# Bulk loads issued by GpSimd, one transposing DMA per attention step, and a column of ones in V

## The reference

```python
x = x + attention(layernorm(x), Wq, bq, Wk, bk, Wv, bv)
x = x + (layernorm(x) @ (weight * scale[:, None]).T + bias)
```

```python
scores = einsum('nhbqd,nhbkd->nhbqk', qb, kb) / sqrt(d)     # local windows
ctx    = einsum('nhbqk,nhbkd->nhbqd', softmax(scores), vb)
_, top_idx = top_k(norm(q), 62);  idx = concat([0, top_idx, t - 1])
ctx[idx] = softmax(q[idx] @ k.T / sqrt(d)) @ v
```

## Time and profile before

| | |
|---|---|
| median of 3 runs | 2244.83 us (2239.55 to 2246.85) |
| the profiled execution | 2241.47 us, span 2239.5 us |
| TensorE busy | 2039.9 us, 91% |
| VectorE, ScalarE, GpSimd busy | 1524.9, 1047.0, 523.3 us |
| attention of the second batch, 600 to 986 us | 386.0 us, TensorE busy 337.06, granted clock 0.92 |
| attention of the fourth batch and what follows, 1530 to 1880 us | 350.0 us, TensorE busy 317.29, granted clock 0.93 |
| linear layer, 1880 to 2239 us | 359.0 us, TensorE busy 355.61, granted clock 1.00 |

### The profile page before, as it was taken

How to read it: one execution, slowest core, us unless ns; L and a number is a source line. 1 busy time by engine, 2 the same in 40 slices (tenths; PEclk the granted TensorE clock), 3 DMA queues, 4 the chain that set the end, 5 groups by cost and what they waited for, 6 DMA issues and landing times.

```text
span 2239.5 us, 37450 instructions
## 1 busy us (share of the span) xinstructions
PE 2039.9 (91%) x11264; PEld 1698.9 (76%) x11264; DVE 1524.9 (68%) x2904; ACT 1047.0 (47%) x1979; POOL 523.3 (23%) x336
## 2 busy tenths in 40 slices
PE   6989797999988879999888699998998997999999
PEld 6877685787867767888677578886887876888887
DVE  6687675774876757748777577577785775666664
ACT  4325555683256646742465466624675682000000
POOL 2241121123321121132321312233222202212221
PEclk9999898999989989999999899999999998999999
DMA  4346656654365566643465556524666645333331
GB/s 154 91 103 132 143 123 117 137 121 130 88 146 129 134 114 124 132 130 113 110 135 138 118 132 132 123 83 97 138 142 169 153 78 166 141 131 127 136 140 66
DMA packets 539680, 280.73 MB, mean 125 GB/s; under 512 B 439120, under 2 KB 504726, under 8 KB 539536
## 3 DMA queue, kind: packets, MB, share of 16 engines
q1 hardware_dynamic: 531888, 261.21, 49.0%
q10 hardware_dynamic: 4320, 15.73, 1.7%
q0 software_dynamic: 3328, 2.17, 0.5%
HBM read 122.73 MB, written 51.44 MB: 78 GB/s over the span
## 4 chain that ended last, share of the span: by engine, by line
PE 47%; DVE 18%; DMA 11%; ACT 9%; issue 8%; SPq 6%; DVEq 1%; ACTq 0%; POOL 0%; POOLq 0%
PE proj L639 20%; PE proj L799 15%; DMA p_turned<-p_parts 7%; PE pv L757 4%; ACT pT L1127 4%; SPq L295 3%; DVE x_norm L1454 3%; ACT probs L1105 3%; DVE top_val L1450 2%; DVE p_parts L1496 2%; DVE top_idx L1452 2%; PE score L771 2%; DVE q_sq L1416 2%; DMA stat_rows<-ln_rstd 1%; PE pv L779 1%
## 5 line engine op out<-in xcount | busy, mean ns | idle before, releaser
L639 PE MATMUL proj<-xT_hi,w_hi 128*128 128x512 f32 x1536 | 447.2, 438 | 99.5 <-ACT vT L1075 79.9
L639 PEld LDWEIGHTS proj<-xT_hi,w_hi 128*128 128x128 f32 x1536 | 302.5, 207 | 169.3 <-ACT vT L1075 83.2
L639 PE MATMUL proj<-xT_hi,w_lo 128*128 128x512 f32 x1536 | 425.8, 407 | 0.0
L500 POOL CAST w_hi<-w_raw 128x1024 fp32r<-128x1024 f32 x96 | 114.2, 1189 | 1225.4 <-PE proj L639 1147.6
L639 PE MATMUL proj<-xT_lo,w_hi 128*128 128x512 f32 x1536 | 381.9, 391 | 0.0
L1127 ACT COPY pT<-p_turned 128x1024 uint16<-128x1024 uint16 x256 | 344.0, 1362 | 71.5 <-DMA p_turned<-p_parts 71.5
L639 PEld LDWEIGHTS proj<-xT_hi,w_lo 128*128 128x128 f32 x1536 | 291.6, 196 | 62.9
L639 PEld LDWEIGHTS proj<-xT_lo,w_hi 128*128 128x128 f32 x1536 | 288.5, 188 | 63.7
L1496 DVE COPY p_parts<-probs 128x1024 uint16<-128x1024 uint16 x320 | 259.4, 820 | 113.7 <-ACT probs L1105 58.1
L757 PEld LDWEIGHTS pv<-v_nat,pT 128*128 128x128 f32 x2048 | 261.5, 201 | 78.1 <-issue 68.2
L757 PE MATMUL pv<-v_nat,pT 128*128 128x64 f32 x2048 | 257.2, 281 | 64.8 <-ACT v_nat L1092 64.8
(11 more groups left out here) (169 smaller groups left out, 3068.9 us busy)
## 6 DMA issues: line engine op xcount, KB each, us to landing
w_raw<-in_wstream SPq DMA_DIRECT2D x96, 512.0 KB, 3.8
x_buf<-in_rows SPq DMA_DIRECT2D x55, 512.0 KB, 3.4
q_rows<-pT SPq DMA_DIRECT2D x64, 256.0 KB, 2.4
ctx_rows<-ctx_out SPq DMA_DIRECT2D x128, 128.0 KB, 2.1
q_store<-ctx_rows SPq DMA_DIRECT2D x30, 512.0 KB, 4.1
out<-q_store ACTq DMA_DIRECT2D x30, 512.0 KB, 2.6
q_store<-in_cols SPq DMA_DIRECT2D x28, 512.0 KB, 3.6
p_turned<-p_parts SPq DMA_TRANSPOSE x320, 3.3
```

The source lines that it names most:

```text
L500: pool.tensor_copy(w_hi[b][:, :], w_raw[b][:, :]).then_inc(w_hi_set, 1)
L639: mm = pe.matmul(proj[:, bank, :], w[b][:, k * P:k * P + P], x[:, k, half * HALF:half * HALF + HALF], start=(m == 0), stop=(m == 23), skip ...
```

## The change

- **Loads.** GpSimd issues the loads of weights (`load_slice`, right after the split that frees the buffer), of columns, of the last rows of a batch (tile pair 3) and the first loads of the linear layer. The first row tiles, the transposes, the contexts and the statistics stay with SyncE.
- **Transposes.** `part_p`, `turn_p` and `join_p` handle a whole step: 2048 16-bit columns, 2304 in the global step. `weigh` waits once.
- **Row sums.** v_nat gets a 65th column per head that is one (zero for tokens outside the sequence). The matmul of pT with v_nat gives the row sum as column 64 of each group; `inverses` reads it from PSUM and is now called by `pv_out` and `g_out`. `exps` and `global_exps` have no accumulator; row_sum is gone.
- **Order.** ScalarE makes both halves' exponentials of a step and then the joined copy of the step before; the second half of vT is copied before that of step 1. Row moments, roots, saving and spreading of the statistics come one pair earlier.

```diff
             def turn_p(n, hp, s):
-                for h in range(2):
-                    words = half_words(s, h)
-                    sp.wait_ge(p_parted, 2 * i + h + 3)
-                    sp.wait_ge(pT_set, 2 * i + h + 1)
-                    sp.dma_start_transpose(p_turned[:, 2 * words.start:2 * words.stop]..., p_parts[...]).then_inc(p_moved[h], 16)
+                sp.wait_ge(p_parted, i + 2)
+                sp.wait_ge(pT_set, i + 1)
+                sp.dma_start_transpose(p_turned[:, 0:2 * words].rearrange("p (x r) -> p x r", r=P),
+                                       p_parts[:, 0:2 * words]).then_inc(p_moved, 16)
...
             def stores(n, hp, following):
-                if next_slices:
-                    sp.wait_ge(w_split[0], n * BUFS + PAIRS // 2 + 3 + hp)
-                    sp.dma_start(w_raw[0][:, :], next_slices[0]).then_inc(raw_in[0], 16)
...
-                if hp < 2 and following:
-                    load_rows(n, hp + 2)
-                if hp == 2:
-                    load_last_column(n, following)
-                if last and not following:
-                    load_first()
                 turn_p(n, hp, 2)
...
                 turn_p(n, hp, 3)
+                if hp == HALF_PAIRS - 1:
+                    if following:
+                        spread_stats(n)
...
-                if hp == HALF_PAIRS - 1 and following:
+                if hp == HALF_PAIRS - 2 and following:
                     save_stats(n)
```

```diff
+            def load_slice(n, i, count):
+                b = i % 2
+                pool.wait_ge(w_split[b], count + 2)
+                apart(pool)
+                pool.dma_start(w_raw[b][:, :], wstream[(i + 2) % SLICES]).then_inc(raw_in[b], 16)
+            def load_rows(n, j):
+                for b in range(2):
+                    pool.wait_ge(rows_seen, n * TILES + 2 * j + b - 1)
+                    pool.dma_start(x_buf[:, b, :], rows_in[n * TILES + 2 * j + b + TILES]).then_inc(last_rows_loaded[b], 16)
...
+                load_column(n, 0)
+                if following:
+                    load_rows(n, 3)
+                for hp in range(PAIRS - 2):
+                    j = hp + 2
+                    split_pair(n, "v", j, load=following or j < PAIRS - 1)
...
+                    split_pair(n, "k", j, load=following or j < PAIRS - 1)
...
+                    load_column(n, hp + 1)
```

```diff
-        v_nat = sb("v_nat", [P, TILES + 1, 2, HD])
+        v_nat = sb("v_nat", [P, TILES + 1, 2, HD + 1])
...
-                            mm = pe.matmul(pv[:, g * HD:g * HD + HD], pT_of(s)[:, ...],
+                            mm = pe.matmul(pv[:, g * (HD + 1):(g + 1) * (HD + 1)], pT_of(s)[:, ...],
                                            v_nat[:, 2 * s + b + c, h, :], start=(c == 0), stop=(c == 1))
...
             def inverses(u, s):
-                dve.wait_ge(exp_set, 2 * (u * EVENTS + s + 1) + 2)
-                dve.reciprocal(row_inv[:, 4 * s:4 * s + size], row_sum[:, 4 * s:4 * s + size]).then_inc(inv_set, 1)
+                dve.wait_ge(pv_done, u * EVENTS + s + 1)
+                sums = pv[:, 0:size * (HD + 1)].rearrange("p (g d) -> p g d", g=size)[:, :, HD]
+                dve.reciprocal(row_inv[:, 4 * s:4 * s + size], sums).then_inc(inv_set, 1)
...
-                if following and hp < HALF_PAIRS - 1:
-                    row_moments(n, hp + 1)
+                if following and hp < HALF_PAIRS - 2:
+                    row_moments(n, hp + 2)
```

318 lines of the change are left out of this document (150 added, 168 removed).

## The result

The changed kernel takes 2265.9 us (median of 4 runs, 2262.0 to 2271.0), the kernel before 2245.8 in the same series: the ratio is 1.0092, with an interval of 1.0071 to 1.0114. It is slower, by 0.9%; forecast were 2100 us. The profiled execution took 2271.0 us.

A forecast was written before the change was run, and what follows sets the result against it. Bound taken: TensorE's work plus waits on the probabilities' way. From 2241.5 us, three batches -129, the fourth -15, last pair -6, columns +6, start +2, together -142, gave 2100 us; forecast 2075 to 2125, range 2050 to 2180.

The forecast's parts named there:

- What bounded the kernel: Whole kernel: TensorE's work plus waits on the probabilities' way; about 58 us in each of three batches, 26 in the fourth.
- Bulk loads: Loads moved from SyncE to GpSimd: 0 on the path for GpSimd's issuing, 1.0 us a pair for overlapping a transpose.
- The loop: Whole-step landing, joined copy and hand-offs: 37.1 us a pair, same as TensorE's own, taken as 38.1 with one load.
- the start: Two weight loads beside the first row tiles: 2 us lost, 0 to 3 possible.
- the end: Last pair, where 8.2 us stood behind four loads ahead of a transpose: 6 of 10 us taken back.
- the opening pairs: First pair of a batch: 40 us taken, against 47.9 before; 42 in the fourth batch's sum.
- The order on ScalarE: vT's second half copied ahead of the joined copy: TensorE's wait for vT over in every pair, the transposes late next.
- Ones column: Extra columns in TensorE's matmuls with v_nat: 6 us more, all on the path; from nothing to twice that.
- Statistics: Saved and spread one pair earlier: pair 4's 13.4 us wait goes, 6 us charged for pair 3.
- Rival 2: Large transpose lands in 5.3 us, a pair 4.1 us longer: 2198 us; chance 0.13.
- Rival 3: Transposes pay their whole cost twice, 6.6 and 7.2 us: 2359 us, slower than before; turn at 5.7 us landing; chance 0.06.
- Rival 4: GpSimd and VectorE hinder each other: 3 DMAs of about 1.05 us a pair hold VectorE, 2142 us; chance 0.10.

The follow-up runs named there:

- in halves: Changed kernel with plain DMAs in 256 B pieces, steps cut in two again, vT's second half copied at its old place in pair 6 alone: 2121.0 us, 0.9435.
- in whole steps: Changed kernel with plain DMAs in 256 B pieces for transposes, vT's second half copied at its old place in pair 6 alone: 2192.7 us, 0.9783.
- The measured phases: No attention, only 512 KB SBUF copies by SyncE, whole or halved, alone or beside bulk loads, eight phases of six: whole and alone landed in 4.1 us.

## Why the prediction was wrong

*What bounded the kernel* was read rightly: waits on the way of the probabilities, and the waits for vT and v_nat in pairs 1 and 4. At these places they are gone in the changed kernel.

*Bulk loads.* Taking them off SyncE gives 25 us. That they cost GpSimd nothing held. What failed is the term of 1.0 us a pair for one load beside a transpose. Alone, one load adds 2.3 us to a copy and two add 3.7; in the changed kernel the landings were late by 119 us in all, 3.8 us a pair, and the transposing DMA of the global step landed at 5.5 to 10.5 us in 19 of 32 cases.

*The loop*, "A pair is 4 x (4.5 + 2.55 + 0.25) + (4.8 + 2.85 + 0.25)", was right in its terms: undisturbed, the trace has 4.27 + 2.53 + 0.2 = 7.0 us a step and 4.6 + 2.8 + 0.2 = 7.6 us for the global one, 35.6 us a pair, and the quietest pairs took 37.1 to 38.6 us. The step that failed comes after it: 38.1 us was taken for 24 pairs, as if a loop nearly as long as TensorE's work could still absorb what comes late. It has 37.1 - 35.6 = 1.5 us a pair for that. The 156 periods from one issue to the next in the four batches took 1385 us, where 128 x 7.0 + 28 x 7.6 = 1109 us are undisturbed: 276 us of lateness, some 9 us a pair. Counted in the trace, landings were late by 119 us, and ScalarE began the joined copy late by 55 us. In the 37 periods that VectorE's copy ended, it began late by 118 us (93 of them in the global step, behind the last piece of V) and was long by 32 us. The four make 324 us; the 48 above 276 are the 1.3 us by which VectorE's copy is shorter than ScalarE's, 37 times, lateness that costs nothing. The sum against the forecast closes so: the seven distances of all batches take 1272.5 us and not 823.8 + 270.6 = 1094.4, +178; the start +7; the stretches between batches, with the ones column charged elsewhere, -1; the end -13; that is 171, and 2271 - 2100 = 171. Of the 178, the four pairs 6 hold 68 us, the pairs 3 hold 27, the opening pairs 10 and the others, with their loads, 72.

*The order on ScalarE.* The prediction priced what is late behind the vT copy no longer waited for, and not what the copy itself waits for. In pair 6 it waits for TensorE, ahead of a joined copy. Its return to the old place gave pair 6 back 5 to 8 us in halves and 6 to 16 in whole steps, and the sum had no term for it.

*Ones column.* The +6 us were not there: 282 ns a matmul with 64 and with 65 columns.

*Statistics.* The place was right, the charge for pair 3 too small, 10 us where 6 were taken. The small writes land as late as before (11.2 us by the median, against 10.9 in the earlier trace rows).

*Rivals.* Rival 2 (the loop sets the pace, 2198 us) had the mechanism, and put it on a landing of 5.3 us. The mean landing was 5.1 us; but the loads, VectorE and ScalarE came on top. Rival 3 put the turn to slower on landings alone, at 5.7 us for all of them; that mean was not reached, and the turn came by lateness of all kinds. It should have been told as one sum: how much lateness a pair, from wherever, eats the 142 us; 142 / 28 is 5 us. The row that could have said so is in the earlier trace rows: TensorE still waited 1.1 us in a quiet pair of the kernel before.

*Rival 4.* VectorE's copies are held by GpSimd, but by its splits: the copy for the global step took 3.56 us in 11 of 32 cases and 2.2 us in 5, 1.35 when alone, and the one shown above began 0.25 us after a split's subtraction and ended 1.2 us after it. It costs 28 us of the 32 in the sum above. The Trainium skill ("SBUF — State Buffer", Who interferes with whom) says that whichever of the two comes second blocks for the whole of the first's instruction; this row agrees. The other half of the rival, that issues of GpSimd hold VectorE for 1.05 us each, is in no row: a bulk load is issued in 0.56 us by the median. It is VectorE that holds them. Of the 136 bulk loads that GpSimd issued, four took 1.18 to 1.30 us, and each of the four began within 0.3 us after the start of a copy to p_parts and ended 0.1 us after its end, as at 813.40 above; the copies kept their 1.35 or 1.23 us.

The Trainium skill ("DMA: Bandwidth & Descriptors", SWDGE vs HWDGE vs iDMA) says that each DMA engine serves the queues of both kinds in turn. The measured phases don't contradict that, but they show what it is worth to the transfer that is waited for: a copy that lands in 4.1 us alone and a load begun with it land at 6.4 and 4.2 us. No phase has the load alone; in the kernel before such loads landed in 3.8 us, so here it is the copy in small pieces that pays.

## What to carry to other kernels

Before two transfers are merged into one, draw the loop through their buffers: if landing, copy and issue form a closed ring, the merged form costs as much as the sum of its parts, and its slack is what is left against the engine that sets the pace, 1.5 us a pair here. If lateness is more than that, it is hidden no longer, and bulk loads on another queue become part of the path. Count the waits of the engine that sets the pace as well as adding them up: many short ones can cost more in slow work behind them than they save in idle time. An instruction moved ahead in an engine's order has to be asked in each unrolled case what it will itself wait for.

## What the runs showed of the hardware

- A plain copy of 512 KB in SBUF in 256 B pieces landed 4.1 us after its issue, half of it 3.0 us. With one 512 KB load begun by GpSimd just ahead the copy landed at 6.4 us, with a second begun 0.5 us behind its issue at 7.8; with one or two issued by SyncE ahead of it at 5.8 and 6.8, counted from the copy's own issue.
- SyncE needs 0.6 us to issue such a copy and 1.3 to 7.1 us for a transposing DMA of the same size: 1.9 us by the median and 3.2 at most where no bulk load of GpSimd was in flight before the landing, 3.1 and 7.1 with two.
- Four issues of bulk loads by GpSimd that began just behind a VectorE copy of 1.2 to 1.35 us took 1.18 to 1.30 us instead of 0.56; the copies were not longer.
- Two kernels whose undisturbed transfers differ by 0.17 us (4.27 transposing, 4.10 plain) differed by 51 us in the sum of 160 landings.
- A matmul of 65 columns took as long as one of 64, 282 ns in the mean of 2048.
- TensorE lost more time in a kernel in which it waited less: 7.5 us less idle, 64 us more of work at the lower of its two clock levels.
